# Putting the first batch of a soft-MoE front among the last groups of an attention stage, in one step list per engine

## The chip, the cores and the metric

The kernel runs on one core of a Trainium2 chip. The metric is device time in microseconds (us). The engines are TensorE (PE in the profile, with PEld for its weight loads), VectorE (DVE), ScalarE (ACT), GpSimd (POOL) and SyncE (SP), which only issues DMAs. Each engine works through its own instructions in program order and waits on semaphores for the others.

## What is computed

Eight sequences of 512 tokens and 256 channels go through an attention block and a soft mixture of experts, each followed by a residual add and a layer norm. Cut to what matters:

```
x1  = layernorm(x + attention(x))          # 16 heads of 32 latent channels, rope, causal
z   = layernorm(x1) * norm_g + norm_b
se  = layernorm(slot_embeds) * ...         # 16 experts x 64 slots
lg  = z @ se.T                             # logits, per batch 512 tokens x 1024 slots
dispatch = softmax over the experts of lg  # for the slots
combine  = softmax over all slots of lg    # for the tokens
slots    = dispatch.T @ z
eout     = (gelu(slots @ Wg) * (slots @ Wu)) @ Wd
out = layernorm(x1 + combine @ eout)
```

## The kernel before

There are four stages, one after the other: attention for batches 0 to 7 (to about 624 us of the span), the front of the mixture for batches 0 to 7 (norm, transposes, logits, both softmaxes, the slots), the 16 experts, and the combine with the last norm. The change concerns the first two and the seam between them.

**Attention.** A batch has four groups of four heads. A group's steps, by name: `lat` (latent q and k), `wqk`, `max` (six units of scores, whose row maxima DVE takes), `neg` (the transposed negated maxima), `exp` (six units of scores again, which ACT exponentiates into `pt`), `mask` (POOL clears the triangle), `pv` (four steps into `ybank`), `y` and `yT` (copy and transpose). A batch ends with `yTT` (transposes), `cproj` (the output projection), `ln` (norm statistics on DVE, 21 short instructions, most in a chain) and `apply` (eight ACT instructions, L757), after which SP stores x1 and the normed `z` to DRAM (L438, L439). Below, (7,2,5) is batch 7, group 2, unit 5.

**Order.** `attn_order(at)` (L43) gives each step a time in slots, 32 a batch and 8 a group plus an offset by name and engine (`PE_AT`, `ACT_AT`, `DVE_AT`, `POOL_AT`, `SP_AT`), and sorts. Each engine issues its own list. PE writes into PSUM: a ring of three two-bank tiles (`ring`, filled in turn), and a fourth, `tail`, whose banks are `misc` and `ybank`. A fill waits until the step that used the tile three fills earlier has been drained by ACT or DVE.

**The front.** `front_order` (L70) goes through a window of steps, one window a batch, with hand-written orders `PE_FRONT`, `ACT_FRONT`, `DVE_FRONT` and `SP_FRONT`, and PE now turns through four tiles (`quad`), `tail` among them. Steps: `zT` (8 transposes of z, L1326; DVE scales them into `xn`, L1037), `xn` (ACT copy L771 and DVE difference L1042, the high and low halves), `zh` (ACT L777 and POOL's `zl` L639), `s1` n (the logits of 128 tokens: 12 matmuls by the helper at L361 to L363, four such pieces a batch; DVE maximum L1046; ACT copy L781 and exponential L782), `c2` and `s2` (8 transposes each of the exponentials and the logits, L1365 and L1348), `s2` further with DVE maxima L1055 and ACT exponentials L788, `e2` (DVE L1062), `d` (transposes L1355, ACT L799, DVE L1070), `slots` (48 matmuls, DVE L1079), `rows` (L1051). A window holds zT and s1 of the batch after the one whose c2, s2, d and slots it makes; window -1 holds zT, xn, zh, s1 and rows of batch 0 alone.

**The seam.** The front's SBUF tiles lie over those of attention. Before its first step SP waits for all eight batches' stores and only then loads z of batch 0:

```
sp.wait_ge(z_stored, B * 16)
sp.wait_ge(x1_stored, B * 16)
load_z(0)
```

PE waits until all PSUM tiles are drained (L1311 to L1314). POOL's `zl` steps are a loop after its attention list (L637 to L640).

Of the kernel before, what the change touches and what calls it, by code (L numbers as in the profile page):

```python
# [41 lines left out]
def attn_order(at):  # L42
# [6 lines left out]
    for b in range(B):  # L49
        for name in at:  # L50
# [43 lines left out]
def block_kernel(nc, a, out):  # L94
# [73 lines left out]
    mts = [place(f"mts{i}", [2 * GH, T], f32r) for i in range(2)]  # L168
    va = place("va", [P, NT, H, L], f32)
# [4 lines left out]
    temp_at = at[0]  # L174
    pt = [place(f"pt{i}", [P, GH, T], f32) for i in range(2)]
    ys = place("ys", [P, T], f32)
    ytok = place("ytok", [P, NT, C], f32)
    yT_ = place("yT_", [P, NC, T], f32)
    x = [place(f"x{i}", [P, NT, C], f32) for i in range(2)]
    x1 = place("x1", [P, NT, C], f32)  # L180
# [26 lines left out]
    s1s = [place(f"s1s{i}", [P, NT, E * S], f32) for i in range(2)]  # L207
    c1 = [place(f"c1{i}", [P, NT, E * S], f32) for i in range(2)]
# [53 lines left out]
    quad = ring + [tail]  # L262
# [9 lines left out]
    pair_filled = [sem(f"pair_filled{r}") for r in range(RING)]  # L272
    pair_drained = [sem(f"pair_drained{r}") for r in range(RING)]
# [15 lines left out]
    quad_filled = [sem(f"quad_filled{r}") for r in range(QUAD)]  # L289
    quad_drained = [sem(f"quad_drained{r}") for r in range(QUAD)]  # L290
# [90 lines left out]
    with nc.Block() as block:  # L381
# [3 lines left out]
        def _(sp):  # L385
# [24 lines left out]
            for st in attn_order(SP_AT):  # L410
# [1075 lines left out]
```

## Time and profile before

| | us |
|---|---|
| median of 3 runs | 1336.6 (1336.46 to 1337.25) |
| the profiled execution, its own time | 1336.36 |
| its span | 1334.5 |
| PE busy | 1215.3 (91%) |
| DVE busy | 814.2 (61%) |
| ACT busy | 682.2 (51%) |
| POOL busy | 449.5 (34%) |
| mean granted TensorE clock | 0.96 |

The span is what the rows are placed in; the execution takes 1.9 us more around it. [...] In the page's 40 slices (33.4 us each) PE shows 9 tenths in most, 7 and 3 in the two slices from 567 to 634 us and 7 in the one after: that is the end of attention and the start of the front.

### The profile page before, as it was taken

Reading aid. Unit: us, or ns where it says so; the run is one execution under the profiler, and the core shown is the slowest. Engines: PE = TensorE matmul, PEld = TensorE weight load, DVE = VectorE, ACT = ScalarE, POOL = GpSimd, SP = SyncE. Lnnn points to the kernel's source line nnn. Section 1 sums busy time; section 2 is a strip of 40 time slices with the busy share of each in tenths; the row PEclk is TensorE's granted clock in tenths of the full one; section 3 lists DMA queues with packets and bytes.
Section 4 is the critical chain, followed back from the end, with each engine's and each line's share of the span. In section 5 each row is a group of like instructions: output and inputs, shape, how many; then the busy total and the mean of one; then the engine's idle time right before and its main releaser. Section 6 shows DMA issues by size and latency. Waiting matters only on the chain.

```text
span 1334.5 us, 19895 instructions
## 1 busy us (share of the span) xinstructions
PE 1215.3 (91%) x7190; PEld 944.3 (71%) x7222; DVE 814.2 (61%) x1318; ACT 682.2 (51%) x1042; POOL 449.5 (34%) x336
## 2 busy tenths in 40 slices
PE   5798999999999999973799999994999999999996
PEld 4465666666656666632688888883888888888885
DVE  3877697979787978631577777763444444432343
ACT  2545464646465656451667777762555555540111
POOL 5544555555545555410100000000444444430000
PEclk9898999999999999976899999997999999999998
DMA  3644353636363645411123333234554545453661
GB/s 121 139 104 111 90 158 87 163 90 159 89 157 91 158 97 134 107 49 63 48 95 111 111 112 112 96 104 152 195 165 166 164 166 165 165 193 95 225 247 47
DMA packets 121790, 170.30 MB, mean 128 GB/s; under 512 B 47025, under 2 KB 76146, under 8 KB 121714
## 3 DMA queue, kind: packets, MB, share of 16 engines
q1 hardware_dynamic: 120818, 168.74, 43.4%
q8 instruction: 46, 0.75, 0.2%
q10 hardware_dynamic: 896, 0.56, 0.1%
q14 instruction: 30, 0.25, 0.1%
HBM read 72.26 MB, written 37.75 MB: 82 GB/s over the span
## 4 chain that ended last, share of the span: by engine, by line
PE 51%; DVE 3%; ACT 2%; DMA 1%; issue 1%; POOL 1%; SPq 0%; ACTq 0%; POOLq 0%; DVEq 0%
PE ring L361 8%; PE ring L363 8%; PE ring L362 7%; PE ring L1438 6%; PE tail L361 3%; PE tail L363 3%; PE tail L362 3%; PE tail L1438 2%; PE ring L1365 2%; PE ring L1348 1%; PE ring L1355 1%; PE tail L1285 1%; PE ring L1274 1%; PE ring L1307 1%; PE tail L1355 1%
## 5 line engine op out<-in xcount | busy, mean ns | idle before, releaser
L738 ACT ACTIVATE pt<-ring 128x1024 f32<-128x1024 f32 (+1 forms) x192 | 169.2, 882 | 148.7 <-PE ring L1274 137.1
L983 DVE TENSOR_REDUCE mx<-ring 128x4 f32<-128x512 f32 (+2 forms) x192 | 197.7, 1039 | 77.6 <-PE ring L1259 77.3
L628 POOL TENSOR_SCALAR_AFFINE_SELECT pt<-pt 128x512 f32<-128x512 f32 x128 | 81.2, 634 | 248.2 <-ACT pt L738 248.2
L1274 PE MATMUL ring<-qks 98*128 98x256 f32 (+3 forms) x512 | 131.6, 361 | 10.3 <-DVE mx L983 4.8
L1257 PE MATMUL ring<-qks 96*128 96x384 f32 (+3 forms) x512 | 139.9, 362 | 0.9 <-DVE mx L983 0.6
L1274 PEld LDWEIGHTS ring<-qks 98*128 98x128 f32 x512 | 77.6, 195 | 69.1 <-DVE mx L983 28.8
L1285 PE MATMUL tail<-pt,va 128*32 128x512 f32 (+3 forms) x1024 | 99.8, 463 | 11.6 <-POOL pt L628 9.8
L653 POOL TENSOR_TENSOR hl<-hid,hh 128x512 fp32r<-128x512 f32 x64 | 82.6, 1302 | 78.4 <-ACT hh L824 78.4
L639 POOL TENSOR_TENSOR zl<-z,zh 128x1024 fp32r<-128x1024 f32 x8 | 19.3, 2410 | 242.9 <-ACT zh L777 242.9
L1257 PEld LDWEIGHTS ring<-qks 96*128 96x128 f32 x512 | 92.2, 199 | 10.9 <-ACT pt L738 6.1
L1097 DVE SCALAR_TENSOR_TENSOR hid<-ring,bias_e,gate 128x512 f32<-128x512 f32 x64 | 47.9, 748 | 83.3 <-ACT gate L818 51.9
L1438 PE MATMUL ring<-eo,c 128*128 (+1 forms) x384 | 88.1, 379 | 0.0
L614 POOL TENSOR_TENSOR rope<-rope,rot 128x1024 f32<-128x1024 f32 x32 | 76.2, 2380 | 30.4 <-DVE rope L973 30.3
L645 POOL TENSOR_TENSOR wul<-wu,wuh 128x1024 fp32r<-128x1024 f32 x16 | 40.6, 2537 | 134.1 <-ACT wuh L812 134.1
L609 POOL TENSOR_TENSOR rot<-rot,sin 128x1024 f32<-128x1024 f32 x32 | 76.6, 2394 | 13.7 <-DVE rot L965 13.7
L818 ACT ACTIVATE gate<-ring,bias_e 128x512 f32<-128x512 f32 x64 | 44.1, 689 | 70.4 <-PE ring L363 64.7
L1438 PEld LDWEIGHTS ring<-eo,c 128*128 128x128 f32 x384 | 72.9, 190 | 9.9
L1259 PE MATMUL ring<-maskb,identb 128*128 128x128 bf16 (+1 forms) x320 | 78.0, 244 | 0.0
L361 PE MATMUL tail<-wdh,hh 128*128 128x256 f32 x256 | 73.3, 286 | 4.3 <-POOL hl L653 4.3
L689 ACT ACTIVATE lat<-ring,blat 128x512 f32<-128x512 f32 x64 | 40.2, 680 | 69.4 <-PE ring L363 58.5
L858 ACT ACTIVATE y<-y,nmr,r 128x256 f32<-128x256 f32 x32 | 16.6, 589 | 112.8 <-DVE nmr L1164 112.8
L362 PE MATMUL tail<-wdh,hl 128*128 128x256 f32 x256 | 73.1, 286 | 0.0
(217 smaller groups left out, 3114.0 us busy)
## 6 DMA issues: line engine op xcount, KB each, us to landing
qks<-stg SPq DMA_DIRECT2D x384, 128.0 KB, 2.4
c_dram<-c2s SPq DMA_DIRECT2D x32, 512.0 KB, 5.2
c<-c_dram SPq DMA_DIRECT2D x32, 512.0 KB, 5.9
sl_dram<-sls SPq DMA_DIRECT2D x32, 256.0 KB, 3.4
sl<-sl_dram SPq DMA_DIRECT2D x16, 512.0 KB, 4.8
wg<-in_wg SPq DMA_DIRECT2D x16, 512.0 KB, 5.6
wu<-in_wu SPq DMA_DIRECT2D x16, 512.0 KB, 6.2
wd<-in_wd SPq DMA_DIRECT2D x16, 512.0 KB, 7.0
```

What stands on the lines that cost most here:

```text
L361: nc.tensor.matmul(dst, lh, rh, start=first, stop=False)
L362: nc.tensor.matmul(dst, ll, rh, start=False, stop=False)
L363: return nc.tensor.matmul(dst, lh, rl, start=False, stop=last)
L628: nc.gpsimd.affine_select(out=m, in_=m, compare_op=ALU.is_ge, fill=0.0, base=0, pattern=[[0, GH], [1, P]], channel_multiplier=-1).then_inc ...
L653: nc.gpsimd.tensor_tensor(out=hl[:, f, :], in0=hid[f % 2][:, :], in1=fp(hh[:, f, :]), op=ALU.subtract).then_inc(hid_low, 1)
L738: nc.scalar.activation(pt[j % 2][:, h:h + heads, 0:n], heads_of(tile, heads, n), ACT.Exp, scale=SCALE).then_inc(empty, 1)
L983: nc.vector.tensor_reduce(out=mx[:, g, i, h:h + heads], in_=heads_of(tile, heads, (i + 1) * P), axis=AX.X, op=ALU.max).then_inc(empty, 1)
L1257: nc.tensor.matmul(scores[:, h, :], qks[0:KS_ROWS, g, h0 + h, 0, i * P:(i + 1) * P], qks[0:KS_ROWS, g, h0 + h, 1, 0:n], start=(h == k), st ...
L1259: last = nc.tensor.matmul(scores[:, k:k + some, i * P:n], identb[:, :], maskb[:, 0:some, :], start=False, stop=True)
L1274: last = nc.tensor.matmul(scores[:, h, :], qks[0:KS_ROWS + 2, g, h0 + h, 1, j * P:(j + 1) * P], qks[0:KS_ROWS + 2, g, h0 + h, 0, j * P:T], ...
L1285: last = nc.tensor.matmul(ybank[h * L:(h + 1) * L, j * P:T], va[:, j, g * GH + h, :], pt[j % 2][:, h, 0:T - j * P], start=(j == 0), stop=( ...
L1438: last = nc.tensor.matmul(acc[i][t // 2][:, t % 2, 0:DO], c2[i][:, n, t * P:(t + 1) * P], eo[:, n, b, :], start=(n == 0), stop=(n == NS - 1))
```

## The change

Attention and front become one list per engine, on PE, ACT, DVE and SP (POOL's `zl` loop stays behind its attention list). `order(at, window, start)` adds the windows of the front at `start + 16.3 * (w + n/len)` slots (start is 264 on PE and SP, 263 on ACT, 261 on DVE), and from window 0 on 18 slots later. So window -1 (`zT`, `s1` of batch 0) lies from slot 247.7 to 264 on PE, which is among groups 1 to 3 of batch 7 (slots 232 to 271), and window 0 begins at 282, behind `cproj` of batch 7 (279). `fills` hands out the PSUM tiles for both: three until the last `misc` or `pv` step, and then also `tail`. The part of each list around the seam is now:

```
PE:  max(7,2,5) cproj 6, zT 0, exp(7,1,2) max(7,3,0) pv(7,1,0) exp(7,1,3) max(7,3,1) ... exp(7,2,1) max(7,3,5)
     exp(7,2,2) s1(0,0) pv(7,2,0) exp(7,2,3) s1(0,1) neg(7,3) exp(7,2,4) s1(0,2) pv(7,2,1) yT(7,1) exp(7,2,5)
     s1(0,3) pv(7,2,2) exp(7,3,0) ... yTT 7, cproj 7, zT 1, c2(0,0) c2(0,1) s2(0,0) s2(0,1) s2(0,2) d(0,0) ...
DVE: max(7,2,4) zT 0, max(7,2,5) negmax(7,2) cproj 6, max(7,3,0) max(7,3,1) xn 0, max(7,3,2) yT(7,0) ln 6,
     max(7,3,3) to max(7,3,5) negmax, s1(0,0) s1(0,1) s1(0,2) yT(7,1) s1(0,3) rows 0, yT(7,2) yT(7,3) cproj 7,
     zT 1, s2(0,0) s2(0,1) s2(0,2) ln 7, e2(0,0) xn 1 ...
ACT: exp(7,1,2) xn 0, exp(7,1,3) ... zh 0, exp(7,2,0) exp(7,2,1) y(7,1) exp(7,2,2) s1(0,0) exp(7,2,3) neg(7,3)
     s1(0,1) exp(7,2,4) apply 6, s1(0,2) exp(7,2,5) s1(0,3) exp(7,3,0) exp(7,3,1) y(7,2) ... yTT 7, c2(0,0)
     ... zh 1, d(0,0) d(0,1) s2(0,3) d(0,2) apply 7, s1(1,0) s1(1,1) d(0,3) ...
SP:  stack(7,3) z 0, store 6, x 7, z 1, c2(0,0) c2(0,1) store 7, z 2, slots(0,0) ...
```

In `SP_FRONT` the load of z two batches on moves from the start of a window to behind `slots(-1,1)`. The SBUF tiles of attention are placed in another order, so that z, xn and their halves (36 KB) lie over the transposed x and the latent and v weights, s1s and c1 of batch 0 over the rope buffers and `stg`, and c2s, e2 and dh over `qks` group by group; each first write gets a wait for the last reader of what lies below. The waits at the seam are gone. The core of the diff (the renamed semaphores, `quad_*` to `pair_*`, and the moved `place` lines are left out):

```diff
+FRONT_AT, FRONT_ACT_AT, FRONT_DVE_AT, FRONT_SPAN, FRONT_GAP = 264, 263, 261, 16.3, 18
...
-def attn_order(at):
+def order(at, window=(), start=FRONT_AT):
...
+    for w in range(-2, B + 1):
+        for n, (name, ahead, *more) in enumerate(window):
+            if 0 <= w + ahead < B:
+                todo.append((start + FRONT_SPAN * (w + n / len(window)) + (FRONT_GAP if w >= 0 else 0), len(todo), (name, w + ahead, *more)))
     return [step for _, _, step in sorted(todo)]
 
 
-def front_order(window):
-
-    steps = []
-    for w in range(-1, B + 1):
-        for name, ahead, *n in window:
-            if 0 <= w + ahead < B:
-                steps.append((name, w + ahead, *n))
-    return steps
+def fills(steps):
+
+    free, left = list(range(RING)), [0] * QUAD
+    slot_of, turn_of = {}, {}
+    last = max(n for n, s in enumerate(steps) if s[0] in MISC_STEPS + ("pv",))
+    for n, s in enumerate(steps):
+        if n == last:
+            free.insert(0, RING)
+        if s[0] in PAIR_STEPS:
+            r = free.pop(0)
+            free.append(r)
+            slot_of[s], turn_of[s] = r, left[r]
+            left[r] += 1
+    return slot_of, turn_of, left
...
-SP_FRONT = (("z", 2), ("c2", 0, 0), ("c2", 0, 1), ("slots", -1, 1), ("slots", 0, 0), ("c2", 0, 2), ("c2", 0, 3))
-
-PAIR_STEPS = ("lat", "max", "exp", "v", "yTT", "cproj", "wv", "seT")
+SP_FRONT = (("c2", 0, 0), ("c2", 0, 1), ("slots", -1, 1), ("z", 2), ("slots", 0, 0), ("c2", 0, 2), ("c2", 0, 3))
+
+PAIR_STEPS = ("lat", "max", "exp", "v", "yTT", "cproj", "wv", "seT", "zT", "s1", "s2", "d", "c2", "slots")
...
+    pe_steps = order(PE_AT, PE_FRONT)
+    slot_of, turn_of, FILLS = fills(pe_steps)
+    misc_no = {s: n for n, s in enumerate(s for s in pe_steps if s[0] in MISC_STEPS)}
...
+    s1s, c1, dh, dl = [], [], [], []
+
+    def rows_of(i):
+        s1s.append(place(f"s1s{i}", [P, NT, E * S], f32))
+        c1.append(place(f"c1{i}", [P, NT, E * S], f32))
+
+    def dispatch_of(i):
+        dh.append(place(f"dh{i}", [P, NT, 512], f32r))
+        dl.append(place(f"dl{i}", [P, NT, 512], f32r))
+
+    assert at[0] <= xt_at + 36 * KB
+    rows_of(0)
+    c2s = [place(f"c2s{i}", [P, 2, T], f32) for i in range(2)]
     e2 = [place(f"e2{i}", [P, 2, T], f32) for i in range(4)]
-    dh = [place(f"dh{i}", [P, NT, 512], f32r) for i in range(2)]
-    dl = [place(f"dl{i}", [P, NT, 512], f32r) for i in range(2)]
-    c2s = [place(f"c2s{i}", [P, 2, T], f32) for i in range(4)]
+    dispatch_of(0)
+    rows_of(1)
+    dispatch_of(1)
+    c2s += [place(f"c2s{i + 2}", [P, 2, T], f32) for i in range(2)]
     sls = [place(f"sls{i}", [P, NC, 512], f32) for i in range(2)]
...
+    def last_read(engine, g):
+        read = ("exp", B - 1, g, len(EXP_UNITS) - 1)
+        engine.wait_ge(pair_filled[slot(read)], fill_count(read))
...
+            def load_z(b):
+                sp.wait_ge(z_stored, (b + 1) * 16)
+                sp.dma_start(z[b % 2][:, :, :], z_dram[b, :, :]).then_inc(z_loaded[b % 2], 16)
+
+            for st in order(SP_AT, SP_FRONT):
...
+                elif name == "z":
+                    if b < 2:
+                        for read in (("lat", B - 1, G - 1), ("v", B - 1)):
+                            sp.wait_ge(pair_filled[slot(read)], fill_count(read))
...
+            for st in order(ACT_AT, ACT_FRONT, FRONT_ACT_AT):
                 name, b = st[:2]
-                if st in pair_no:
-                    tile = ring[slot(st)]
+                if st in slot_of:
...
+                    if (b, n) == (0, 0):
+                        act.wait_ge(cosed, B * G)
+                        act.wait_ge(roped, B * G)
+                        act.wait_ge(k_low, B * G)
+                        act.wait_ge(misc_filled, misc_count(("wqk", B - 1, G - 1)))
+                        for g in range(G):
+                            act.wait_ge(stacked[g], B * 3 * GH * 16)
+                    elif (b, n) == (1, 0):
+                        last_read(act, G - 1)
+                        act.wait_ge(y_filled, B * G)
...
+                    if b == 0 and n < 2:
+                        last_read(act, 0)
+                    elif b == 0:
+                        act.wait_ge(y_filled, B * G)
+                        act.wait_ge(misc_filled, misc_count(("yT", B - 1, G - 1)))
...
+            for st in order(DVE_AT, DVE_FRONT, FRONT_DVE_AT):
                 name, b = st[:2]
-                if st in pair_no:
-                    tile = ring[slot(st)]
+                if st in slot_of:
...
+            for st in pe_steps:
                 name, b = st[:2]
                 if name in PAIR_STEPS:
-                    tile = ring[slot(st)]
+                    tile = pairs[slot(st)]
                     full = pair_filled[slot(st)]
                     pe.wait_ge(pair_drained[slot(st)], fill_count(st, 0))
+                    if (slot(st), fill_count(st)) == (RING, 1):
+                        pe.wait_ge(misc_drained, len(misc_no))
+                        pe.wait_ge(y_drained, B * G)
...
-                pe.wait_ge(pair_drained[r], FILLS[r])
-            pe.wait_ge(misc_drained, len(misc_no))
-            pe.wait_ge(y_drained, B * G)
-
-            for st in front_steps:
-                name, b = st[:2]
-                tile = quad[quad_slot(st)]
-                full = quad_filled[quad_slot(st)]
-                pe.wait_ge(quad_drained[quad_slot(st)], quad_count(st, 0))
-
-                if name == "zT":
+                elif name == "zT":
```

## Rows read from the trace of the kernel before

**Rows 1.** Busy time of each engine by stretch (us); PEclk: granted clock.

```profile
core 0: us, PE busy (x) PEld busy (x) DVE busy (x) ACT busy (x) POOL busy (x), PEclk, DMA share, GB/s
...
591.00:614.70 23.70, 17.91 (x86) 11.07 (x86) 1.36 (x4) 6.53 (x9) 4.91 (x6) 0.64 0.18 62
614.70:637.70 23.00, 1.95 (x9) 1.61 (x9) 7.84 (x25) 6.04 (x10) 0.35 (x1) 0.61 0.24 92
637.70:655.10 17.40, 14.76 (x56) 11.89 (x56) 4.90 (x4) 8.47 (x12) 2.11 (x1) 0.83 0.09 31
655.10:662.60 7.50, 4.56 (x40) 4.36 (x41) 6.20 (x10) 6.23 (x14) 0.00 (x0) 1.00 0.35 140
662.60:687.10 24.50, 22.95 (x128) 19.45 (x129) 18.05 (x26) 16.32 (x30) 2.43 (x1) 1.00 0.00 1
687.10:722.00 34.90, 34.90 (x218) 30.89 (x217) 24.53 (x38) 25.21 (x44) 2.40 (x1) 1.00 0.35 110
```

**Rows 2.** The chain that ended last, 614 to 664 us: start, us, what.

```profile
614.73 1.23 DVE x L1009
...
624.77 3.55 DMA z_dram<-x
628.34 3.26 DMA z<-z_dram
...
633.67 4.02 issue
...
639.31 0.43 PE ring L361
...
649.77 0.23 PE ring L362
...
658.00 3.49 DVE m L1055 x3
```

**Rows 3.** PE's timeline, 561 to 663 us: start, us, line, tiles, idle before.

```profile
561.57 3.67 PE L1307 MATMUL ring<-cw,yT__105 128*128 128x256 f32 x16
564.89 0.71 PE L1274 MATMUL ring<-qks 98*128 98x384 f32 x2
...
577.22 0.73 PE L1274 MATMUL ring<-qks 98*128 98x512 f32 x2 [2.61 <-DVE mx L983]
...
594.08 1.93 PE L1285 MATMUL tail<-pt,va 128*32 128x512 f32 x8 [1.48 <-POOL pt L628]
...
609.21 5.48 PE L1307 MATMUL ring<-cw,yT__105 128*128 128x256 f32 x16 [1.21 <-ACT yT__105 L751]
...
651.43 1.03 PE L1326 MATMUL ring<-ident,z 128*128 128x128 f32 x8
...
662.62 1.06 PE L1355 MATMUL tail<-ident,e 128*128 128x128 f32 x8 [2.92 <-DVE e L1062]
```

**Rows 4.** DVE's timeline, the same columns, 561 to 644 us.

```profile
561.77 1.22 DVE L983 TENSOR_REDUCE mx<-ring 128x2 f32<-128x1024 f32 x1 [0.48 <-PE ring L1259]
...
576.21 2.08 DVE L983 TENSOR_REDUCE mx<-ring 128x2 f32<-128x768 f32 x2
...
633.71 1.53 DVE L1037 TENSOR_SCALAR xn<-ring,ng,nb__52 128x512 f32<-128x512 f32 x2 [13.42 <-PE ring L1326]
...
643.19 1.23 DVE L1046 TENSOR_REDUCE m<-ring 128x1 f32<-128x1024 f32 x1 [5.60 <-PE ring L363]
```

**Rows 5.** ACT's timeline, the same columns, 592 to 646 us.

```profile
592.24 1.02 ACT L738 ACTIVATE pt<-ring 128x1024 f32<-128x1024 f32 x1 [0.97 <-PE ring L1274]
...
620.33 4.04 ACT L757 ACTIVATE x<-x,nmean,ny 128x256 f32<-128x256 f32 x8 [11.26 <-DVE nmean L1024]
...
644.45 1.03 ACT L781 ACTIVATE s1s<-ring 128x1024 f32<-128x1024 f32 x1 [7.17 <-DVE m L1046]
645.37 1.11 ACT L782 ACTIVATE c<-ring,m 128x1024 f32<-128x1024 f32 x1
```

**Rows 6.** SP's timeline before the seam.

```profile
550.49 7.68 SPq L435 DMA_DIRECT2D qks<-stg  x12
```

More of the change, by code:

```diff
@@ L151, in block_kernel @@
     wvl = place("wvl", [P, NC, C], f32r)
-    wq = place("wq", [P, P], f32)
-    cw = place("cw", [P, NC, C], f32)
+    lat = place("lat", [P, 2, T], f32)
+    rot = place("rot", [P, 2, T], f32)
+    rope = place("rope", [P, 2, T], f32)
     cos = place("cos", [P, T], f32)
     sin = place("sin", [P, T], f32)
-    blat = place("blat", [P, 2, G], f32)
+    stg = [place(f"stg{i}", [P, 4, T], f32r) for i in range(2)]
+    qks = place("qks", [P, G, GH, 2, T], f32r)
+    mts = [place(f"mts{i}", [2 * GH, T], f32r) for i in range(2)]
+    identb = place("identb", [P, P], bf16)
+    maskb = place("maskb", [P, GH, P], bf16)
+    wq = place("wq", [P, P], f32)
     bwq = place("bwq", [P, 1], f32)
     bv = place("bv", [P, C], f32)
+    va = place("va", [P, NT, H, L], f32)
+    temp_at = at[0]
+    pt = [place(f"pt{i}", [P, GH, T], f32) for i in range(2)]
+    ys = place("ys", [P, T], f32)
+    ytok = place("ytok", [P, NT, C], f32)
+    yT_ = place("yT_", [P, NC, T], f32)
+    x = [place(f"x{i}", [P, NT, C], f32) for i in range(2)]
+    x1 = place("x1", [P, NT, C], f32)
+    cw = place("cw", [P, NC, C], f32)
+    blat = place("blat", [P, 2, G], f32)
     cpb = place("cpb", [P, C], f32)
@@ L173, in block_kernel @@
     snv, sny, snt, snm = (place(n, [P, 8], f32) for n in ("snv", "sny", "snt", "snm"))
[L174 to L180, printed above, removed]
+    m1 = place("m1", [P, 2, NT], f32)
+    cs = place("cs", [P, 2, NT], f32)
+    m2 = place("m2", [P, NT, 2], f32)
+    es = place("es", [P, NT, 2], f32)
+    res = place("res", [P, NT, 2], f32)
     at[0] = temp_at
@@ L261, in block_kernel @@
     misc, ybank = tail[:, 0, :], tail[:, 1, :]
-    quad = ring + [tail]
+    pairs = ring + [tail]
     acc = ((ring[0], ring[1]), (ring[2], tail))
@@ L271, in block_kernel @@
     setup_dve = sem("setup_dve")
-    pair_filled = [sem(f"pair_filled{r}") for r in range(RING)]
-    pair_drained = [sem(f"pair_drained{r}") for r in range(RING)]
+    pair_filled = [sem(f"pair_filled{r}") for r in range(QUAD)]
+    pair_drained = [sem(f"pair_drained{r}") for r in range(QUAD)]
     misc_filled, misc_drained = sem("misc_filled"), sem("misc_drained")
@@ L602, in _ @@
             pool.wait_ge(in_rope, IN_ROPE * 16)
-            for st in attn_order(POOL_AT):
+            for st in order(POOL_AT):
                 name, b = st[:2]
@@ L758, in _ @@
                     last.then_inc(applied, 1)
-            for st in front_order(ACT_FRONT):
-                name, b = st[:2]
-                if st in quad_no:
-                    tile = quad[quad_slot(st)]
-                    full, empty = quad_filled[quad_slot(st)], quad_drained[quad_slot(st)]
-                if name == "xn":
-                    act.wait_ge(quad_drained[quad_slot(("zT", b))], quad_count(("zT", b)))
+                elif name == "xn":
+                    act.wait_ge(pair_drained[slot(("zT", b))], fill_count(("zT", b)))
                     if b:
@@ L986, in _ @@
                     g = st[2]
-                    for r in range(RING):
+                    for r in range(QUAD):
                         done = [fill_count(s) for s in (("max", b, g, u) for u in range(len(MAX_UNITS))) if slot(s) == r]
@@ L1025, in _ @@
                                                    in1=ny[:, :, :], op0=ALU.mult, op1=ALU.mult).then_inc(ln_ready, 1)
-            assert chain[0] == B * ATTN_CHAIN, chain[0]
-            for st in front_order(DVE_FRONT):
-                name, b = st[:2]
-                if st in quad_no:
-                    tile = quad[quad_slot(st)]
-                    full, empty = quad_filled[quad_slot(st)], quad_drained[quad_slot(st)]
-                if name == "zT":
-                    dve.wait_ge(full, quad_count(st))
+                elif name == "zT":
+                    dve.wait_ge(full, fill_count(st))
                     dve.wait_ge(xn_low, b)
@@ L1067, in _ @@
                     dve.wait_ge(d_high, 2 * (b * NT + n + 1))
+                    if b == 0 and n < 2:
+                        last_read(dve, 2)
+                    elif b == 0:
+                        dve.wait_ge(y_filled, B * G)
                     cols = slice(n % 2 * 256, n % 2 * 256 + 256)
@@ L1075, in _ @@
                     h = st[2]
-                    dve.wait_ge(full, quad_count(st))
+                    dve.wait_ge(full, fill_count(st))
                     dve.wait_ge(sl_stored[h], b * NC * 16)
+                    if b == 0:
+                        read = ("cproj", B - 1)
+                        dve.wait_ge(pair_filled[slot(read)], fill_count(read))
                     for d in range(NC):
@@ L1309, in _ @@
                     last.then_inc(full, 1)
-            for r in range(RING):
-                pe.wait_ge(pair_drained[r], FILLS[r])
-            pe.wait_ge(misc_drained, len(misc_no))
-            pe.wait_ge(y_drained, B * G)
-            for st in front_steps:
-                name, b = st[:2]
-                tile = quad[quad_slot(st)]
-                full = quad_filled[quad_slot(st)]
-                pe.wait_ge(quad_drained[quad_slot(st)], quad_count(st, 0))
-                if name == "zT":
+                elif name == "zT":
                     pe.wait_ge(z_loaded[b % 2], (b // 2 + 1) * 16)
```

87 lines of the change are left out of this document (27 added, 60 removed).

## The prediction, made before the changed kernel ran

> **What bounds the kernel now.** I read the page first: PE is the busiest engine and its weak slices lie at the seam. Then busy time by stretch, which shows how weak: PE works 1.95 us of the 23.0 between the end of the last `cproj` and the first logits, 14.8 of the next 17.4 and at a granted clock of 0.83, and 17.9 of the 23.7 before the seam, at 0.64 [rows 1]. Windows 0 and 1 of the front are PE-bound (22.95 of 24.5, 34.9 of 34.9) at full clock [rows 1]. So what is worth anything is PE's time between 614.7 and 662.6.
>
> The chain of waits says what fills it: `cproj` is drained, norm statistics run, `apply` of batch 7, z of batch 7 goes to DRAM (3.55), z of batch 0 comes back (3.26), then zT, its halves (4.02 under "issue"), the logits, at half clock at first (0.43 a matmul against 0.23 later), the softmax [rows 2, 5]. Batch 0 needs none of batch 7; it is queued behind it. d(0,0), the first step behind which PE is full again, starts at 662.62 [rows 3].
>
> **The change, part by part,** as a timetable from the same execution. Work is not removed: it moves.
>
> *a. zT 0 stalls DVE's queue.* z 0 is issued behind the twelve `stack` DMAs of group (7,3), the last at about 558.2 [rows 6], and its load takes 3.3, so it lands at 562, before PE is through `cproj` 6 at 561.57 + 3.67 = 565.1 [rows 3]. That load is hidden, with 3 us to spare. But DVE's list has zT 0 ahead of max(7,2,5) and of the drain of `cproj` 6, while PE issues zT 0 behind both. Now DVE takes max(7,2,5) at 561.77 [rows 4]. Then it waits for zT 0, which PE makes from 565.1 to 566.0 (0.9 to the next start; the row says 1.03 with the tail of the last) [rows 3]; DVE's part takes 1.53, then the maximum 1.22 [rows 4], end 568.8. PE's next step, exp(7,1,2), needs the tile of max(7,2,5): it starts at 568.8 and not at 564.89 [rows 3], 3.9 later. max(7,3,0) needs the tile of `cproj` 6, whose drain (1.23) [rows 2] comes after that: 5.0 later than now. xn 0 on DVE stands ahead of max(7,3,2), so max(7,3,3), now at 576.21 [rows 4], starts at some 581.6, 5.4 later. PE sits idle some 4 us in two pieces. Now an idle piece of 2.61 us [rows 3] was followed by a half clock. For a stretch at half clock that isn't there now I take +2.5, with 0 and 4 as bounds.
>
> *b. The logits of batch 0 among groups 2 and 3.* At full clock PE pays 12 x 0.227 = 2.7 a piece, at half 12 x 0.43 = 5.1 [rows 2]; DVE 1.23 [rows 4]; ACT 1.03 + 1.11 = 2.14 [rows 5]. With three tiles in the ring each piece holds one until ACT is through, and ACT has its pieces before exp(7,2,3), exp(7,2,4), exp(7,2,5) and exp(7,3,0). From the first piece on ACT's list is full: four pieces 8.6, `apply` 6 4.0 (it is there now too), the exponentials. So ACT pays all of 4 x 2.14 = 8.6. Ahead of it stands the first piece on PE and DVE, for which I count 4.6 + 1.2 less what ACT and PE wait anyway, 3.2 net. xnh and zh (one copy of 1024 columns each, as the 1.03 of [rows 5]) fall into ACT's idle time, and the `rows` step into DVE's. Thus exp(7,3,1), on ACT at 592.24 now [rows 5], comes 5.4 + 8.6 + 3.2 = 17.2 later, at 609.4.
>
> *c. The rest of group 3 and `cproj` 7* are the steps of now in the order of now, 592.24 to 614.7. Between them PE waits for masks and copies, the clock stays as low as it is now, 0.64 [rows 1], and they last as long. `cproj` 7 ends 17.2 + a's clock, of which half survives in ACT's full stretch: 18.5 later, at 633.2. Bounds 11 and 25.
>
> *d. From `cproj` 7 to d(0,0).* All of z's way and batch 0's logits is gone from here. PE goes on without a gap: zT 1, c2, c2, s2 are 4 x 0.9 and a little for the first at half clock, 3.9; the three s2 maxima 3.5 [rows 2]. `ln` 7 now stands on DVE between them and e2(0,0): from the end of the x drain (615.96) to `apply` (620.33), 4.4 [rows 2, 5]. It was hidden by nothing and is paid here. e2(0,0) is 1.1: 13.0 in all, where there are 662.62 - 614.7 = 47.9 now. Gain 34.9. z 1 (behind store 6 and x 7 on SP, some 605) lands 20 us early; bias 7 on POOL stands before the drain with 10 us of room; `zl` 0 stays behind bias 7 and is needed by slots(0,0) 30 us later. Each is hidden by the length of group 3; without that z 1 would cost its 3.3.
>
> *e. After d(0,0).* `apply` 7 (4.04) [rows 5] now stands on ACT ahead of s1(1,0), which holds a tile that d(0,3) needs, so slots(0,0) comes 2.8 later (bounds 1 and 4). PE had stood idle 7 us before d(0,0), so I take half clock for d, s2, d and part of s1(1,0), of which 1.5 is left once DVE's pace is counted (0 to 3). The new waits on earlier readers all name PE steps that stand well before; price 0. On SP, store 7 waits for `apply` 7 with z 2, slots(0,0) and two c2 stores behind it; z 2 lands some 5 us after `apply`, zT 2 comes 25 later. In each later window z is loaded a third of a window later, of 33 us, and is wanted at the start of the next: room of some 15 us. Window 1 on, experts and combine: unchanged.
>
> Sum: -34.9 + 18.5 + 2.8 + 1.5 = -12.1. Made against the profiled execution, 1336.36 - 12.1 = 1324.3; the median of the three runs is 0.24 above it, so rounded 1324.
>
> **The rivals.** *R1, the clock stays full.* The logits keep PE busy in the last groups; if the clock holds to `cproj` 7, that takes 3.67 and not 5.48 [rows 3], a third less; a third of the 17.9 busy us of the stretch [rows 1] is 6, of which I take 5, as not all of it lies on the chain. a's clock term (1.3 left) and e's (1.5) go too. -12.1 - 7.8 = -19.9: 1316.5. For it: the pieces are longer unbroken work than anything PE has there now. Against: between masks PE is a third idle, as now, and now that goes with 0.64.
>
> *R2, the clock stays half through the transposes.* After `cproj` 7 PE has only transposes until s1(1,0). If they don't bring the clock back, four of them take twice as long, 7.8 and not 3.9, the next two 1.5 over DVE's pace, and e's clock term doubles to 3: +6.9, 1331.2. Now transposes after 655.1 run at full clock [rows 1], but the logits came just before them; and those logits, from 637.7 on, were at half clock still at 639.31 and full at 649.77 [rows 2], so some unbroken work is needed, and `cproj` 7 gives 5.48 of it. [...] No row here shows transposes alone after an idle stretch.
>
> *R3, slower: each logits piece serial with the attention chain.* Place: the three-tile ring in group 2 of batch 7. If PE, DVE and ACT take their parts of a piece one after the other while exp and mask wait, a piece costs 5.1 + 1.2 + 2.1 = 8.4, four 34, with a's 5.4 + 2.5: 42 at the end of `cproj`. +42 - 34.9 + 4.3 = +11: 1347.5. It decides from a delay of `cproj` 7 of over 34.9 - 4.3 = 30.6. Against: the orders give ACT an exp between pieces, and PE can start piece 2 while ACT has piece 1. For: DVE now is idle most of the time there (1.36 busy of 23.7) [rows 1], so this stretch is a chain, not throughput.
>
> *R4, nothing comes of it.* The seam closes, but the last groups give all back: the delay of `cproj` 7 is some 30. It would need a second stall like a's.
>
> **How the numbers follow.** Forecast 0.50, its own range 1318 to 1330 from the bounds of a, c and e. R1 0.22, R2 0.13, R3 0.09, R4 0.06. The predicted time is the forecast's. The range, 1311 to 1335, takes in R1 and R2 with their bounds and leaves R3 and the slower part of R4 out. 0.2% (2.7 us) is what a measurement of this kernel can tell from no change. Faster: forecast, R1, R2, 0.85; same: R4, 0.06; slower: R3, 0.09.
>
> **What would show it.** DVE idle from 561.3 to 566 and exp(7,1,2) at 568.8 (a). ACT nearly full between s1(0,0) and exp(7,3,0), with exp(7,3,1) at 609 (b). `cproj` 7 of 5.5 us, ending at 633 (c; 3.7 us at 625 is R1; past 645 R3). PE idle under 10 us from there to d(0,0) at 646, with `ln` 7 as the releaser's neighbour (d). apply 7 ahead of s1(1,0) and slots(0,0) ending some 27 us after d(0,0) began, where it is under 24.5 now (e). c2 transposes of 1.9 for eight would be R2. I am wrong if later windows of the front show PE waiting for z or for a store, or if a stage behind the front changes its length.

## The result, and the profile after

The changed kernel takes 1323.4 us (1322.98 to 1323.63, four runs) where the kernel before takes 1336.9 on the same chip: a ratio of 0.9897, 95% interval 0.988 to 0.9914. Forecast were 1324 and a range of 1311 to 1335. A second set (experiment 5) gave 1321.8 against 1338.4, 0.9877 (0.9856 to 0.9898). The profiled execution has a span of 1321.3, 13.2 less than before.

Busy time of the changed kernel in the stretches that answer to [rows 1]: the full part of the last groups, the rest of them with `cproj` 7, from there to d(0,0), window 0 to its last transposes, and window 1.

```profile
core 0: us, PE busy (x) PEld busy (x) DVE busy (x) ACT busy (x) POOL busy (x), PEclk, DMA share, GB/s
585.55:609.90 24.35, 21.30 (x109) 14.45 (x110) 9.24 (x12) 16.88 (x26) 2.54 (x4) 0.88 0.14 48
609.90:633.45 23.55, 17.91 (x80) 11.28 (x80) 1.54 (x5) 7.35 (x11) 7.16 (x6) 0.61 0.12 42
633.45:647.88 14.43, 5.24 (x48) 5.03 (x47) 13.08 (x31) 7.95 (x16) 2.34 (x1) 0.79 0.18 73
647.88:672.62 24.74, 23.11 (x113) 19.75 (x114) 14.86 (x23) 17.61 (x32) 0.00 (x0) 0.92 0.17 64
672.62:707.50 34.88, 34.88 (x217) 30.87 (x216) 25.32 (x39) 24.52 (x43) 2.39 (x1) 1.00 0.32 106
```

The stretch of 23.0 us in which PE worked 1.95 is gone. In its place 14.4 us lie between `cproj` 7 and d(0,0), in which DVE is busy 13.1: the bound has moved to DVE. The last part of attention is what it was, to the second digit of PE's busy time (17.91) and nearly in its clock (0.61 against 0.64). Window 1 has its 34.9 us of before.

PE's timeline of the changed kernel at the places that answer to [rows 3] (start, us, line, tiles, idle before):

```profile
563.32 3.67 PE L1336 MATMUL ring<-cw,yT__85 128*128 128x256 f32 x16
566.83 1.04 PE L1343 MATMUL ring<-ident,z 128*128 128x128 f32 x8
570.62 1.01 PE L1303 MATMUL ring<-qks 98*128 98x384 f32 x2 [2.75 <-DVE mx L1009]
...
586.55 0.73 PE L1303 MATMUL ring<-qks 98*128 98x512 f32 x2 [2.92 <-DVE mx L1009]
...
612.83 1.93 PE L1314 MATMUL tail<-pt,va 128*32 128x512 f32 x8 [1.44 <-POOL pt L639]
...
627.97 5.48 PE L1336 MATMUL ring<-cw,yT__85 128*128 128x256 f32 x16 [1.21 <-ACT yT__85 L762]
633.29 1.04 PE L1343 MATMUL ring<-ident,z 128*128 128x128 f32 x8
...
647.88 1.94 PE L1372 MATMUL tail<-ident,e 128*128 128x128 f32 x8 [9.19 <-DVE e L1081]
649.62 1.91 PE L1365 MATMUL ring<-ident,s1s 128*128 128x128 f32 x8
651.32 1.41 PE L1372 MATMUL ring<-ident,e 128*128 128x128 f32 x8
652.49 0.47 PE L376 MATMUL ring<-seh,xnh 128*128 128x512 f32 x1
652.80 0.39 PE L377 MATMUL ring<-seh,xnl 128*128 128x512 f32 x1
```

Eight 128x128 transposes take 1.04 us at the clock's upper level (the row of 633.29) and 1.91 at half clock (649.62). The granted clock was 1.00 in window 1, and 0.50 while such transposes ran from 654.62 to 659.63 in experiment 4.

Since the lists are the same up to there, I measure from the start of `cproj` 6 (561.57 before, 563.32 here). The 1.75 between them need not be the change's: in the second profile of the changed kernel (experiment 5) `cproj` 6 starts at 561.50. From that point to the end of the span it is 772.9 us before, 758.0 in the changed kernel and 758.3 in its second profile: the change is worth 14.9 by this profile and 14.6 by the other. Where it goes, in us:

| step | before | changed | difference | forecast |
|---|---|---|---|---|
| a: `cproj` 6 to exp(7,1,2) on PE | 3.3 | 7.3 | +4.0 | +3.9 |
| a: `cproj` 6 to max(7,3,3) on DVE | 14.6 | 22.2 | +7.6 | +5.4, with clock +7.9 |
| a, b: `cproj` 6 to exp(7,3,1) on ACT | 30.7 | 47.7 | +17.0 | +17.2 |
| a to c: `cproj` 6 to the drain of `cproj` 7 | 53.2 | 70.2 | +17.0 | +18.5 |
| d: that drain to d(0,0) | 47.9 | 14.4 | -33.5 | -34.9 |
| e: d(0,0) to c2(0,2) | 22.7 | 24.7 | +2.0 | +4.3 |
| the rest | 649.1 | 648.7 | -0.5 | 0 |

The stretch that was forecast full on ACT, on ACT's timeline of the changed kernel; eight neighbouring rows of it, without the two of 0.2 that read the accumulator:

```profile
600.76 1.02 ACT L749 ACTIVATE pt<-ring 128x1024 f32<-128x1024 f32 x1
601.66 4.04 ACT L768 ACTIVATE x<-x,nmean,ny 128x256 f32<-128x256 f32 x8
605.60 1.01 ACT L796 ACTIVATE s1s<-ring 128x1024 f32<-128x1024 f32 x1
606.51 1.11 ACT L797 ACTIVATE c<-ring,m 128x1024 f32<-128x1024 f32 x1
...
607.60 0.59 ACT L749 ACTIVATE pt<-ring 128x512 f32<-128x512 f32 x1
608.07 1.02 ACT L796 ACTIVATE s1s<-ring 128x1024 f32<-128x1024 f32 x1
608.98 1.12 ACT L797 ACTIVATE c<-ring,m 128x1024 f32<-128x1024 f32 x1
...
610.06 1.95 ACT L749 ACTIVATE pt<-ring 128x1024 f32<-128x1024 f32 x2
```

None of them has an idle time before it. The two exponentials that begin at 610.06 are exp(7,3,0) and exp(7,3,1).

### The profile page after: what moved, and what is told of

Same layout as the page of the kernel before. It is cut to its first block, busy times and chain, and to the rows that moved or that the text cites. A ratio compares the mean times of both kernels' runs of the same rounds, so it can differ in the third digit from the quotient of the medians.

```text
span 1321.3 us, 19946 instructions
## 1 busy us (share of the span) xinstructions
PE 1221.5 (92%) x7222; PEld 945.8 (72%) x7222; DVE 814.6 (62%) x1318; ACT 681.2 (52%) x1042; POOL 449.7 (34%) x336
## 4 chain that ended last, share of the span: by engine, by line
PE 51%; DVE 3%; ACT 2%; POOL 1%; issue 1%; DMA 1%; ACTq 0%; SPq 0%; POOLq 0%; DVEq 0%
PE ring L376 7%; PE ring L377 7%; PE ring L378 7%; PE ring L1455 6%; PE tail L376 3%; PE tail L378 3%; PE tail L377 3%; PE tail L1455 2%; PE ring L1382 2%; PE ring L1365 2%; PE ring L1372 1%; PE tail L1314 1%; PE tail L1372 1%; PE ring L1336 1%; PE ring L1303 1%
## 5 line engine op out<-in xcount | busy, mean ns | idle before, releaser
L664 POOL TENSOR_TENSOR hl<-hid,hh 128x512 fp32r<-128x512 f32 x64 | 82.6, 1301 | 77.6 <-ACT hh L850 77.6
L1286 PEld LDWEIGHTS ring<-qks 96*128 96x128 f32 x512 | 93.4, 202 | 11.8 <-ACT pt L749 6.5
L1123 DVE SCALAR_TENSOR_TENSOR hid<-ring,bias_e,gate 128x512 f32<-128x512 f32 x64 | 47.9, 748 | 83.9 <-ACT gate L844 49.7
L1288 PE MATMUL ring<-maskb,identb 128*128 128x128 bf16 (+2 forms) x352 | 92.3, 262 | 0.0
```

The costliest lines, as they stand in the source:

```text
L664: nc.gpsimd.tensor_tensor(out=hl[:, f, :], in0=hid[f % 2][:, :], in1=fp(hh[:, f, :]), op=ALU.subtract).then_inc(hid_low, 1)
L1286: nc.tensor.matmul(scores[:, h, :], qks[0:KS_ROWS, g, h0 + h, 0, i * P:(i + 1) * P], qks[0:KS_ROWS, g, h0 + h, 1, 0:n], start=(h == k), st ...
L1288: last = nc.tensor.matmul(scores[:, k:k + some, i * P:n], identb[:, :], maskb[:, 0:some, :], start=False, stop=True)
```

## The experiments

Ten variants ran, and the changed kernel once more. Each was timed beside the kernel before, whose median lay between 1337.7 and 1338.4 there; the ratios are to that. All variants but the third start from the changed kernel and move steps in the lists by one more argument:

```diff
-def order(at, window=(), start=FRONT_AT):
+def order(at, window=(), start=FRONT_AT, move={}):
-    return [step for _, _, step in sorted(todo)]
+    return [step for _, _, step in sorted((move.get(step, slot), n, step) for slot, n, step in todo)]
```

**1. The drain of zT 0 behind that of `cproj` 6, on DVE.**

```diff
+MOVE_DVE = {("zT", 0): 245.603}
```

> One part undone: on DVE alone, the drain of zT 0 moves from ahead of max(7,2,5) to behind the drain of cproj 6. Theory (the wait at zT 0 costs 4.0 us and then a stretch at half clock, and the rest of the last groups only shifts): PE's 2.75 us wait before exp(7,1,2) is gone, max(7,3,3) comes 5 to 7 us earlier, and the kernel gains 4 to 6 us on the 1323.4 of the changed kernel: 1317.5 to 1319.5. Rival (ACT's full stretch sets the end of the last groups whatever happens before it): max(7,3,3) comes earlier, but the end of cproj 7 hardly moves, 0 to -1.5 us.

1318.0 us, ratio 0.9854 (0.9833 to 0.9876). Its four runs end at 1319.2, those of the changed kernel on the same chip begin at 1320.6. PE's timeline of this run:

```profile
564.64 1.04 PE L1344 MATMUL ring<-ident,z 128*128 128x128 f32 x8
565.43 0.60 PE L1304 MATMUL ring<-qks 98*128 98x384 f32 x2
...
578.30 1.22 PE L1304 MATMUL ring<-qks 98*128 98x512 f32 x2 [2.91 <-DVE mx L1010]
```

The wait of 2.75 is gone, exp(7,1,2) follows zT 0 at once, and the next wait, for max(7,3,3), ends 17.2 us after the start of `cproj` 6 (561.13 here) instead of 23.2. So step a cost 6.1 at that point, of which 3.6 to 4.2 arrive at `cproj` 7 (the step behind it starts 65.7 after `cproj` 6, against 70.0 and, in the second profile, 69.3). The theory holds; the rival, that ACT's full stretch absorbs it, is out. What is lost on the way goes mostly into the first logits piece: after its wait of 2.91 us PE is at half clock at once (1.22 for the two matmuls of the row above, where the changed kernel's take 0.73) and stays there for seven of the piece's twelve matmuls, not four (0.63 us each and 0.56 the last of them, where the rest take 0.39 or 0.40).

**2. Norm 7 out of the way of window 0.**

```diff
+MOVE_DVE = {("ln", 7): 293.3}
+MOVE_ACT = {("apply", 7): 297.0}
+MOVE_SP = {("store", 7): 298.0}
```

> The norm of batch 7 taken out of the way of window 0: ln 7 on DVE moves from ahead of e2(0,0) to ahead of slots(0,0), where DVE stood idle 4.2 us before; apply 7 on ACT from ahead of s1(1,0) to behind c2(0,3), store 7 on SP behind it. Theory (steps d and e: ln 7 lies bare on the way to d(0,0), 6.2 us in the changed kernel, apply 7 costs 2 to 3 behind it, the half clock after the 9.2 us idle 1.5): less 1.9 for a collision with zl 1 that then falls on an e2 as it did before, -6 to -8 us: 1315.5 to 1317.5. Rival (PE waits for something else there, so the time comes back as another wait in window 0 or 1): -3 us or less.

1315.7 us, ratio 0.9832 (0.9812 to 0.9853). PE's timeline of this run:

```profile
640.16 1.74 PE L1375 MATMUL tail<-ident,e 128*128 128x128 f32 x8 [2.91 <-DVE e L1084]
...
662.88 1.91 PE L1385 MATMUL ring<-ident,c 128*128 128x128 f32 x16
...
670.78 1.09 PE L1368 MATMUL ring<-ident,s1s 128*128 128x128 f32 x8 [1.62 <-ACT c2s L833]
```

DVE's timeline of the same run:

```profile
641.26 0.88 DVE L1084 TENSOR_SCALAR e<-e,res 128x512 f32<-128x512 f32 x2
...
642.25 2.78 DVE L1084 TENSOR_SCALAR e<-e,res 128x512 f32<-128x512 f32 x2
```

And POOL's:

```profile
641.95 2.41 POOL L653 TENSOR_TENSOR zl<-z,zh 128x1024 fp32r<-128x1024 f32 x1 [16.75 <-ACT zh L785]
```

PE waits 2.91 before d(0,0), as it did before the change [rows 3], instead of 9.19, and from d(0,0) to c2(0,2) it takes 22.7, as before, not 24.7. Together 8.3 at this place. So steps d and e are shown: `ln` 7 and `apply` 7 lay bare. PE still comes out of its wait at half clock here (1.74 for the eight transposes of d(0,0), 1.06 before the change), so that half clock costs nothing up to c2(0,2): the whole 2.0 was `apply` 7's. Not all of it arrives. From `cproj` 6 to the span's end it is 751.7 (758.0 in the changed kernel, 758.3 in its second profile), 6.6 less: the later `apply` 7 (4.04 from 665.78) holds up c2s on ACT (669.72), and PE waits 1.62 for it in window 1 (the row of 670.78), where the changed kernel has no such wait. An e2 of 2.78 instead of 0.88 beside POOL's `zl` of 2.41 shows the collision that the expectation reckoned with.

**3. Layout alone.** The kernel before, with the `place` lines of the changed kernel and nothing else.

> The kernel before with nothing changed but the order of its SBUF tiles, which is that of the changed kernel. Theory: the place of a tile costs nothing, 1336.9 within 0.7. Rival: the 1.75 us by which attention's batch 6 ends later in the changed kernel's trace comes from the layout, so this one takes 1338 to 1339.

1337.9 us (ten runs), ratio 0.9998 (0.9986 to 1.0009). The new SBUF order costs and gives nothing; it only permits the rest.

**4. The logits of batch 0 behind `cproj` 7.**

```diff
+MOVE_PE = {("s1", 0, n): 279.1 + 0.1 * n for n in range(4)}
+MOVE_DVE = {**{("s1", 0, n): 277.7 + 0.1 * n for n in range(4)}, ("rows", 0): 278.2}
+MOVE_ACT = {("s1", 0, n): 276.2 + 0.1 * n for n in range(4)}
```

> Splits the change in two: zT 0, xn 0 and zh 0 stay in the last groups, but the four logits pieces of batch 0 (and rows 0) move behind cproj 7 on PE, ACT and DVE. Theory (the way of z through DRAM, 7 us, the norm, apply and zT are what is gained; the logits among the groups are paid for by ACT at nearly their own price): cproj 7 ends 8 to 10 us earlier than in the changed kernel, d(0,0) starts 4 to 7 us later, in all +4 to +7: 1327.5 to 1330.5. Rival 1 (the logits' place is the gain): +13, back to 1336. Rival 2 (their place is worth nothing): 1323.4 within 1.5.

1328.1 us, ratio 0.9923 (0.9902 to 0.9944). PE's timeline:

```profile
619.27 5.46 PE L1339 MATMUL ring<-cw,yT__85 128*128 128x256 f32 x16 [1.21 <-ACT yT__85 L765]
...
654.62 1.94 PE L1375 MATMUL tail<-ident,e 128*128 128x128 f32 x8 [9.19 <-DVE e L1084]
```

`cproj` 7 starts 55.6 after `cproj` 6 (563.68), not 64.3 (the mean of the changed kernel's two profiles, 64.7 and 64.0): 8.7 earlier. d(0,0) comes 90.9 after it, not 84.2 (84.6 and 83.9): 6.7 later. From `cproj` 6 to the span's end it is 763.8, 9.1 less than before the change, where the change gives 14.6 to 14.9. So not quite two thirds of the gain come from z of batch 0 being loaded, transposed and split early, and a good third from the place of the logits, for which 8.7 are paid in the groups (ACT's four pieces are 8.6) and 15.4 saved behind them.

**5. The changed kernel again**, the reference of the next three.

> The changed kernel once more, as the reference of the three below on the same chip: 1323.4 within 1, and the time at which cproj 6 starts again apart from 563.3 by up to 2 us, since up to there the kernels run the same list.

1321.8 us, ratio 0.9877. `cproj` 6 at 561.50; from there every place lies within 0.7 of the first profile.

**6. zh 1 later on ACT, and with it `zl` 1 on POOL.**

```diff
+MOVE_ACT = {("zh", 1): 290.1}
```

> On ACT alone zh 1 moves from ahead of d(0,0) to behind d(0,2), and with it POOL's zl 1, from the time of ln 7 to a time when DVE has no instruction with all its inputs in SBUF. Theory (one multiply of the Newton chain, 0.17 us otherwise, took 2.23 because POOL's subtraction of 2.34 started 0.13 before it, and both read SBUF): that row is 0.17 again, ln 7 takes 4.2 as ln 6 does, and the kernel gains 1.5 to 2.2: 1321.2 to 1321.9. Rival (the 2.23 is DVE's own, or the profile's): 0, the row stays. [...]

1323.2 us, ratio 0.9892 (0.9867 to 0.9917), against 1321.8 for the reference: no gain. The mechanism held and the time did not. First the changed kernel's DVE timeline where `ln` 7 runs:

```profile
642.91 0.17 DVE L913 TENSOR_TENSOR nt__100<-nt__100,nv 128x8 f32<-128x8 f32 x1
...
643.51 2.23 DVE L913 TENSOR_TENSOR nt__100<-nt__100,nv 128x8 f32<-128x8 f32 x1
645.78 0.17 DVE L914 SCALAR_TENSOR_TENSOR ny<-nt__100,ny 128x8 f32<-128x8 f32 x1
```

And its POOL timeline there:

```profile
643.38 2.34 POOL L650 TENSOR_TENSOR zl<-z,zh 128x1024 fp32r<-128x1024 f32 x1 [16.76 <-ACT zh L782]
```

This run's PE timeline:

```profile
644.91 1.94 PE L1373 MATMUL tail<-ident,e 128*128 128x128 f32 x8 [7.13 <-DVE e L1082]
...
660.80 1.38 PE L1373 MATMUL ring<-ident,e 128*128 128x128 f32 x8 [2.60 <-ACT c L798]
```

And its ACT timeline:

```profile
653.75 1.06 ACT L783 ACTIVATE zh<-z 128x1024 fp32r<-128x1024 f32 x1
654.70 4.04 ACT L769 ACTIVATE x<-x,nmean,ny 128x256 f32<-128x256 f32 x8
658.64 1.01 ACT L797 ACTIVATE s1s<-ring 128x1024 f32<-128x1024 f32 x1
```

PE's wait before d(0,0) fell from 9.20 in the reference to 7.13, the 2.1 of the blocked multiply. The multiply takes 0.17 in this run and `ln` 7 4.2, so the collision with POOL is shown. But zh 1 now stands on ACT ahead of `apply` 7 and s1(1,0), and d(0,3) waits for s1(1,0)'s tile 2.60 where it waited 1.65. From d(0,0) to c2(0,2) it takes 26.6, not 24.7, and at c2(0,2) both kernels stand at 108.66 after `cproj` 6. The gain was given back inside one window, because ACT was the next bound there.

**7. `apply` 6 later on ACT.**

```diff
+MOVE_ACT = {("apply", 6): 266.2}
+MOVE_SP = {("x", 7): 253.91, ("z", 1): 253.92}
```

> apply 6 on ACT moves from ahead of s1(0,2) to behind exp(7,3,4), where ACT waits 3.1 us; the loads of x 7 and z 1 on SP move ahead of store 6. Theory (between s1(0,1) and exp(7,3,1) ACT is full, and its 4.0 us of apply set the pace): exp(7,3,1) and the end of cproj 7 come 2.5 to 4 earlier, kernel 1319.5 to 1321. Rival 1 (PE and DVE need the time for the pieces anyway): 0 to -1. Rival 2 (apply now delays the last group instead): 0 or slower.

1322.4 us, ratio 0.988 (0.9861 to 0.9899): nothing. ACT's timeline:

```profile
607.08 1.94 ACT L751 ACTIVATE pt<-ring 128x1024 f32<-128x1024 f32 x2
...
612.74 1.88 ACT L751 ACTIVATE pt<-ring 128x768 f32<-128x768 f32 x2 [2.54 <-PE ring L1305]
614.52 4.03 ACT L770 ACTIVATE x<-x,nmean,ny 128x256 f32<-128x256 f32 x8
618.45 0.58 ACT L751 ACTIVATE pt<-ring 128x512 f32<-128x512 f32 x1
```

exp(7,3,0) comes 1.6 earlier after `cproj` 6 (44.5 against 46.1), not 2.5 to 4: with `apply` out of the stretch the logits' own way through PE and DVE is nearly as long. And `apply`, 4.03 long in an idle piece of 3.1, holds exp(7,3,5) up, so that `cproj` 7 starts only 0.2 earlier. Both rivals were half right; my theory of one setter for the stretch fell.

**8. The four moves together.**

> The moves of zT 0, of ln, apply and store 7, of zh 1 and of apply 6 together. Theory (they lie on different stretches of one path, so that the gains add): -5.4 and -7.7 as measured, about 1.9 for zh 1 (its collision would fall on e2(0,2)), about 3 for apply 6: 1304.5 to 1307.5. Rival (they share one slack): 1310 to 1315, no better than the best of them by more than 4.

1307.9 us, ratio 0.9771 (0.9752 to 0.9789), 13.8 under its reference. That is 0.4 above the upper edge of what the theory gave. From `cproj` 6 to the span's end it is 743.8, 14.5 less than the 758.3 of the reference. Alone, by the same measure, the first move gave 4.4 (753.9), the second 6.6 (751.7), zh 1 -0.2 (758.5) and `apply` 6 0.3 (758.0), together 11.1. So in these profiles the four do 3.4 more than apart; the next experiment divides that.

**9. Only the two that paid.**

> Only the two moves that paid by themselves: zT 0 on DVE, and ln, apply and store 7. Theory (they lie on different stretches; zh 1 late and apply 6 late gave nothing alone): -5 and -7 on the changed kernel's 1321.8 to 1323.4, 1309 to 1311, 1 to 3 above the four moves together, because zl 1 falls on e2(0,2) again and apply 6 stands in ACT's full stretch. Rival: the same as the four together, 1307.9 within 0.7.

1311.6 us, ratio 0.979 (0.9768 to 0.9813). From `cproj` 6 to the span's end it is 747.2, 11.1 less than in the reference: just the 4.4 and 6.6 that these two gave apart. The time is 0.6 above the theory's upper edge and 3.7 above the four together, so the rival is out. Where the 3.4 lie: `cproj` 7 starts 59.7 after `cproj` 6 here, 57.7 there, and that 1.9 is `apply` 6, since zh 1 comes later. Of it 0.6 are lost again up to c2(0,2) (36.4 from `cproj` 7 here, 37.0 there, where `cproj` 7 itself ran longer at half clock, 6.36 against 5.51). The other 2.1 lie behind c2(0,2), where the rest takes 651.1 here and 649.0 there, and most of them are the clock's. PE's timeline in the front's last window, in this run:

```profile
880.19 1.61 PE L1375 MATMUL tail<-ident,e 128*128 128x128 f32 x8 [3.04 <-DVE e L1084]
...
888.19 1.91 PE L1385 MATMUL ring<-ident,c 128*128 128x128 f32 x16
```

And in the run with the four moves:

```profile
877.62 1.06 PE L1375 MATMUL tail<-ident,e 128*128 128x128 f32 x8 [3.04 <-DVE e L1084]
...
884.01 1.91 PE L1385 MATMUL ring<-ident,c 128*128 128x128 f32 x16
```

The wait is the same 3.04, but here PE needs 8.0 us for the steps between these rows, at a mean granted clock of 0.79, and there 6.4 at 1.00. With zh 1 late in both, experiment 10 needs 8.0 and experiment 11 6.4; so zh 1 doesn't decide it. That is 1.6 of the 2.1; the rest lies mostly in the next wait, for POOL (16.34 against 15.93). So `apply` 6 is shown to pay once `cproj` 7 is earlier, 1.3 up to c2(0,2); no row shows zh 1 paying.

**10. `apply` 6 behind yTT 7.**

```diff
-MOVE_ACT = {..., ("apply", 6): 266.2}
+MOVE_ACT = {..., ("apply", 6): 276.2}
+MOVE_SP = {..., ("store", 6): 281.5}
```

> The four moves, but apply 6 behind yTT 7 on ACT, where it waits 7.4 us, and store 6 behind it. Theory (in the run of apply 6 alone its 4.0 us was taken from ahead of exp(7,3,1), 1.6 earlier, and put ahead of exp(7,3,5), 1.3 later): now nothing stands behind it, cproj 7 comes 1 to 2 earlier than in the four together, 1306 to 1307. Rival: no change, 1307.9 within 0.7.

1309.5 us (1306.71 to 1312.73), ratio 0.9779 (0.975 to 0.9809). Too wide to tell 1 us; from `cproj` 6 to the end it is 744.6, against 743.8 in the four moves. In the trace `cproj` 7 starts 57.6 after `cproj` 6, as in the four moves (57.7), and its next step 62.6, not 63.9, because it ran less at half clock (5.20 against 6.36). At c2(0,2) this run is 1.3 ahead (93.4 after `cproj` 6, against 94.7), and then loses 2.2, most of it in the last window as told above. Unclear in the time, small in the trace.

**11. `ln` 6 behind negmax(7,3) as well.**

```diff
+MOVE_DVE = {..., ("ln", 6): 253.6}
```

> As the one before, and ln 6 on DVE moves from ahead of max(7,3,3) to behind negmax(7,3), where DVE waits for the first logits. Theory (PE waits 2.9 us for max(7,3,3), which stands behind the 4.2 of ln 6, and falls to half clock over the first piece): the wait goes, cproj 7 comes 3 to 6 earlier, 1301 to 1304. Rival (the logits then wait for ln 6 on DVE instead, and ACT's stretch starts as late): 0 to -1.5, 1305 or more.

1305.9 us (1305.19 to 1306.37), ratio 0.9752 (0.9731 to 0.9774). The best of all: 2.5% under the kernel before, where the change itself gave 1.0 to 1.2%. But the theory's 1301 to 1304 is missed by 1.9. The time lies in the rival's 1305 or more, though 3.6 below the run before and not 0 to 1.5. From `cproj` 6 to the span's end it is 741.0, 17.3 less than in the reference. Busy time from 575 to 600 us, in the columns of the first fence of this document's result; the run before this one:

```profile
575.00:600.00 25.00, 22.10 (x117) 15.17 (x120) 11.78 (x33) 13.39 (x19) 3.18 (x5) 0.86 0.00 1
```

And this run, in the same columns:

```profile
575.00:600.00 25.00, 22.28 (x126) 14.13 (x126) 12.61 (x33) 15.62 (x23) 2.64 (x5) 1.00 0.00 1
```

PE's wait behind `ln` 6 is gone and the clock stays at its upper level throughout this stretch (1.00, against 0.86). `cproj` 7 starts 54.7 after `cproj` 6, 2.9 earlier; a part of the expected 3 to 6 went, as the rival said, into the first logits piece, whose maximum waits for `ln` 6 now (ACT idle 5.59 before it, 4.52 in the run before). At c2(0,2) 1.6 of the 2.9 are left (91.8 after `cproj` 6, against 93.4), because `cproj` 7 ran longer at half clock (6.43 against 5.20). The other 1.9 of the 3.6 by which this profile is shorter than the one before (741.0 against 744.6) lie behind c2(0,2), 1.6 of them the clock in the last window; only the 1.6 ahead of it are the move's.

## Why the prediction was right

The sum came to -12.1 and the profiled execution gained 13.4, the median of the first runs 13.5. Each step was there and each size within 2.3 us. That the total is so near is in part luck: measured from `cproj` 6, the same places give -15.0 (17.0 - 33.5 + 2.0 - 0.5). The forecast was 1.5 too high for c, 2.3 too high for e and 1.4 too good for d, and `cproj` 6 happened to start 1.75 late in this profile.

- **a** was right to 0.1 in its wait (2.75 idle, exp(7,1,2) 4.0 late) and right that a half clock follows, for 573.67 has a 512-wide pv step of 1.94, where that step takes 1.07 in the kernel before (566.15). At max(7,3,3) it comes to 7.6, where the prediction has 5.4 and 2.5 for the clock.
- **b** came to 17.0 for 17.2, but not by its own terms. The prediction has 5.4 at max(7,3,3) and 11.8 behind it; measured are 7.6 and 9.4. And the argument, ACT full and therefore the setter, was only half of it: without `apply` 6 in the stretch exp(7,3,0) moved 1.6, not 4.
- **c** came to 17.0 for 18.5. The steps themselves are exact: 22.5 us from exp(7,3,1) to the drain of `cproj` 7 before and after, at nearly the same clock (0.64 and 0.61). What was mis-sized is how far a and b overlap, and two experiments show it. By the start of `cproj` 7 (47.6 after `cproj` 6 before the change), a without the logits in the groups costs 8.0 (experiment 4, 55.6), and the logits with a's wait undone cost 12.8 (experiment 1, 60.5). Those are nearly the prediction's 7.9 and 11.8. Together they cost 16.4 to 17.0 and not 20.8: some 4 us are absorbed, where the prediction let half of the clock term go, 1.2.
- **d** was 1.4 too good (its terms add to 12.9, not to the 13.0 that the prediction says). `ln` 7 took 6.3, not 4.4, because one of its multiplies ran into POOL's `zl` 1 (2.23 for 0.17). The kernel before paid the same 1.9 in an e2 a little later (2.80 for 0.88 at 664.71, beside POOL's subtraction of 2.43 from 664.40), so the collision was not new; it had moved to a bare place.
- **e** was 2.3 too bad: +2.0 for +4.3. PE did start d(0,0) at half clock (1.94 for its eight transposes), but that is not to be added: in experiment 2 the half clock is still there, nearly as long (1.74, 1.91 and 1.24 for the three groups of eight, against 1.94, 1.91 and 1.41), and the stretch takes its 22.7 of before, in which PE waited 1.34 for DVE's `dl` anyway. The 2.0 are `apply` 7's, for which 2.8 were counted.

The forecast of an unchanged rest held: windows from 1 on take what they took, and the later load of z shows nowhere. R1 is out by `cproj` 7 of 5.48 and a mean granted clock of 0.61 in that stretch; R3 and R4 by a delay of 17.0 against the 30.6 from which they decide. R2 is out by the transposes: the eight at 634.16 behind `cproj` 7 took 1.04 and not 1.9, so the clock was back before they began, and after the 9.19 us of waiting the clock came back while nothing but transposes ran, see below.

What I had not seen is how cheaply step d could be had: I costed `ln` 7 as paid and never asked whether it must stand there. Moving the drain of zT 0 and the norm of batch 7 was worth 11.1 us, three quarters of what the change itself gave (14.6 by the same measure).

## What to carry to other kernels

When two stages are joined in one list, look at every wait that the joint list puts in front of an engine's other work, not only at what it takes away: here a drain ahead of two others cost 4.4 us and a norm ahead of the first softmax 6.6, about a third and nearly a half of the net gain, and both could be read off the lists before any run. A move that gives nothing alone can be worth something once the next bound is out of the way (`apply` 6, 0.3 alone and 1.3 behind the others), so test moves in combination before dropping them. When a combination gives more than its parts, look where the surplus lies: of the 3.4 here 1.6 were the clock after one and the same wait, far from anything that had been moved. And follow the trace from a point where both kernels still run the same list: the first 560 us differed by 1.82 (563.32 against 561.50) between two profiles of one program.

## What the runs showed of the hardware

**The clock came back on transposes alone.** PE waited 9.19 us, then from 647.88 ran three times eight 128x128 fp32 transposes and nothing else: 1.94, 1.91 and 1.41 us, and the first logits matmul behind them already took 0.47 and the next 0.39, as at the upper level (0.48 and 0.40 from 665.57 in the kernel before, where the pair at half clock from 637.69 took 0.77 and 0.63). The time at which it comes back differs: in the fourth experiment all three took 1.9, the first logits matmul still 0.78 and the next 0.48. But some 15 us earlier in that run the clock fell after a wait of 2.69 us and came back within transposes too: of five groups of eight the first two took 1.28 and 1.91 and the last three 3.44 together, where they take 2.78 at the upper level (656.92 in the kernel before). All of these are fp32 transposes as this kernel makes them.

**A 128x8 multiply on DVE took 2.23 us instead of 0.17 beside a subtraction on GpSimd.** It ended at 645.74, when POOL's 128x1024 subtraction ended (643.38 + 2.34). With that subtraction elsewhere the multiply took 0.17 and PE's wait for this chain fell by 2.07 (experiment 6). There the subtraction ran from 654.89 to 657.29, and DVE's instructions beside it, each with an input in PSUM, took 1.28 (two differences of `d`) and 1.22 (a maximum), against 1.29 and 1.23 in the changed kernel without it. A tensor_scalar between SBUF tiles took 2.78 for 0.88 beside such a subtraction (2.41 from 641.95) in experiment 2.
